# A gated Flamingo layer on one core: batch 0's first half in two quarters, with bonus sums by float32 matmuls

## What is computed

```python
def step(carry, kv_t):
    p, q, o = carry
    no = jnp.maximum(o, u + kt)
    A = jnp.exp(o - no); E = jnp.exp(u + kt - no)
    y = (A * p + E * vt) / (A * q + E)
    no2 = jnp.maximum(w + o, kt)
    A2 = jnp.exp(w + o - no2); E2 = jnp.exp(kt - no2)
    return ((A2 * p + E2 * vt, A2 * q + E2, no2), y)
...
x = x + tanh(g_xattn[0]) * wkv(4, 1024, 1024, w, u, layernorm(x), ctx_2048)
D = gelu(float16(layernorm(x)) @ W0.T + bias0).astype(float16)
x = x + tanh(g_ffn[0]) * (D @ W1.T + bias1).astype(float16)
```

## Time and profile before

| | us |
|---|---|
| median of three runs | 1918.29 (1917.05 to 1918.54) |
| the profiled execution, its own time | 1916.53 |
| its span, first to last instruction | 1914.7 |
| first group of half 0 starts | 112.13 |
| first group of half 1 starts | 240.16 |
| mean granted clock of TensorE | 0.998 |

### The profile page before, as it was taken

The page is one execution under the profiler, slowest core; times in us unless marked ns, Lnnn a source line. Parts: engine busy times, 40 slices in busy tenths (PEclk is TensorE's granted clock), DMA queues, the critical chain, the costliest instruction groups (busy, mean ns, idle before and its releaser), DMA issues.

```text
span 1914.7 us, 20205 instructions
## 1 busy us (share of the span) xinstructions
PE 1812.3 (95%) x8408; PEld 829.5 (43%) x8408; DVE 879.1 (46%) x997; ACT 555.7 (29%) x673; POOL 333.9 (17%) x325
## 2 busy tenths in 40 slices
PE   1189899999999999999999999999999999999999
PEld 0144444444444444444444444444444444444444
DVE  8968748898447857633215867742300000000000
ACT  5059534634424434311003434410101221100000
POOL 4336402565211211200001221200000000000000
PEclk9999999999999999999999999999999999999999
DMA  6639776767574443332452443233233212222330
GB/s 247 247 118 327 236 259 232 251 238 267 195 213 143 146 151 133 141 108 104 138 185 106 149 160 137 89 132 128 93 120 132 88 45 88 88 81 95 132 121 34
DMA packets 82953, 291.89 MB, mean 152 GB/s; under 512 B 12583, under 2 KB 12583, under 8 KB 75693
## 3 DMA queue, kind: packets, MB, share of 16 engines
q1 hardware_dynamic: 74940, 177.30, 27.3%
q10 hardware_dynamic: 7920, 113.30, 16.8%
HBM read 223.41 MB, written 67.16 MB: 152 GB/s over the span
## 4 chain that ended last, share of the span: by engine, by line
PE 90%; DVE 1%; ACT 1%; DMA 1%; POOL 1%; issue 1%; SPq 0%; ACTq 0%; DVEq 0%; POOLq 0%
PE accs L903 45%; PE accs L925 44%; POOL W L447 0%; DVE stats L626 0%; DMA var_dram<-tokens 0%; ACT W L555 0%; PE front L861 0%; PE back L870 0%; DMA total<-var_dram 0%; PE front L884 0%; DVE XT L757 0%; PE front L879 0%; DVE xh L673 0%; DMA var_dram<-total 0%; PE front L837 0%
## 5 line engine op out<-in xcount | busy, mean ns | idle before, releaser
L903 PE MATMUL accs<-XT,W 128*128 128x512 f16 x4096 | 888.9, 379 | 4.2 <-ACT XT L527 2.4
L925 PE MATMUL accs<-DT,W 128*128 128x512 f16 x4096 | 886.7, 379 | 0.0
L925 PEld LDWEIGHTS accs<-DT,W 128*128 128x128 f16 x4096 | 400.8, 98 | 487.3 <-issue 6.8
L903 PEld LDWEIGHTS accs<-XT,W 128*128 128x128 f16 x4096 | 400.8, 98 | 486.3 <-issue 5.1
L765 DVE SCALAR_TENSOR_TENSOR xo<-e,tg,xo 128x512 f32<-128x512 f16 x64 | 50.3, 787 | 633.0 <-ACT e L572 633.0
L564 ACT ACTIVATE DT<-accs,small 128x512 f16<-128x512 f32 x256 | 175.6, 686 | 516.0 <-PE accs L903 515.4
L572 ACT ACTIVATE e<-accs,small 128x512 f16<-128x512 f32 x64 | 43.9, 686 | 660.3 <-PE accs L925 660.3
L720 DVE RECIPROCAL S<-front 128x512 f32<-128x512 f32 x64 | 214.4, 3350 | 0.0
L425 POOL TENSOR_TENSOR X<-X,S 128x512 f32<-128x512 f32 x64 | 92.5, 1446 | 521.1 <-DVE S L723 521.1
L447 POOL TENSOR_TENSOR W<-stage,W 128x1024 f16<-128x1024 f32 x52 | 110.6, 2138 | 46.3 <-ACT stage L558 46.3
L706 DVE TENSOR_TENSOR front<-front,V 128x512 f32<-128x512 f32 x64 | 44.5, 696 | 137.6 <-ACT front L522 136.0
(11 more groups left out here) (69 smaller groups left out, 596.1 us busy)
## 6 DMA issues: line engine op xcount, KB each, us to landing
W<-parts_dram ACTq DMA_DIRECT2D x54, 2048.0 KB, 9.2
parts_dram<-W SPq DMA_DIRECT2D x64, 512.0 KB, 5.1
stage<-w_in SPq DMA_DIRECT2D x52, 512.0 KB, 5.7
xin<-x_in SPq DMA_DIRECT2D x32, 512.0 KB, 7.0
V<-vT_in SPq DMA_DIRECT2D x64, 256.0 KB, 5.5
X<-xT_in SPq DMA_DIRECT2D x64, 256.0 KB, 6.6
x_dram<-X SPq DMA_DIRECT2D x32, 512.0 KB, 4.5
xo<-x_dram SPq DMA_DIRECT2D x32, 512.0 KB, 4.3
```

The lines of the kernel that those rows point to most:

```text
L903: mm = nc.tensor.matmul(acc[m % BANKS], W[:, (nb // Q) % 2, part, nb % Q, P * c:P * (c + 1)], XT[:, c, HALF * half:HALF * (half + 1)], sta ...
L925: mm = nc.tensor.matmul(acc[m % BANKS], W[:, s % 2, part, q, P * c:P * (c + 1)], DT[:, nb, HALF * half:HALF * (half + 1)], start=(nb == 0 ...
```

## The change

The first half of batch 0 is worked as two quarters of 256 tokens (`QUARTER`). Units 0 to 7 are the first quarter, 8 to 15 the second, 16 to 23 the second half with 512 tokens.

- **First quarter.** The exp writes to SBUF (`EA`, in `total`), the product also (`EVA`). In place of DVE's two bonus sums TensorE forms them by four float32 matmuls of 256 columns: a diagonal matrix of the bonus (`diag`, made by ACT ahead of the first normalisation, 8 of 128x128) times E, plus the identity times the scan, and the same for the product (`terms`). DVE's order is scan, product, scan of unit n + 1 (`scans_first`), then reciprocal and quotient of unit n (`quotient_first`). 12 weight pieces are made ready beside it, 3 for each two units.
- **Matmul groups.** The first 64 groups (`EARLY`) have 256 columns: 25 of the first quarter, then, behind the second quarter's tiles (slot `SECOND` = 25), 12 of the second quarter, and then one of the first with two of the second in turn, to 64. The 32 groups of half 1 with 512 columns follow (slot `THIRD` = 64). `EXTRA` = 32 slots are added.
- **Tiles.** Their second normalisation stands between groups, not among them: tiles 0 and 1 ahead of slot 0, 2 and 3 at slot 25, 4 to 7 at slot 64. `xh` has two buffers.
- **Weight pieces.** More of them stay in the chip at first: in free parts of X2, XT, DT and W. Each is stored by two transfers, in an order of its own, with 8 semaphores.
- **Slots.** Units 8 to 15 in slots 1 to 13, units 16 to 23 in 31 to 61; POOL's residual has slots of its own (`ADD_SLOT`). Batch 1's units start three slots later in half 1 (43 in place of 40), the last is at the same place.

```diff
+QUARTER = HALF // 2
+LAG = 25
+EARLY = ([(0, nb) for nb in range(LAG)] + [(1, nb) for nb in range(12)] +
+         [x for j in range(NB - LAG) for x in ((0, LAG + j), (1, 12 + 2 * j), (1, 13 + 2 * j))] +
+         [(1, nb) for nb in range(12 + 2 * (NB - LAG), NB)])
+SECOND, THIRD = LAG, len(EARLY)
...
+WITH_UNIT = ((0, 1), (2,), (3, 4), (5,), (6, 7), (8,), (9, 10), (11,))
...
+            for c in range(CB):
+                nc.scalar.activation(diag[c], ident[:, :], ACT.Copy, scale=bonus[:, c:c + 1]).then_inc(diag_done, 1)
...
+            def scans_first(n):
+                j, w, c = n % 2, QUARTER, n
+                E, EV = EA[:, j, :], EVA[:, j, :]
+                S_p, S_q = S[:, j, 0, :], S[:, j, 1, :]
+                dve.wait_ge(seeded, n + 1)
+                dve.wait_ge(e_ready, n + 1)
+                nc.vector.tensor_tensor_scan(S_q[:, 1:w + 1], decay[:, c:c + 1].to_broadcast([P, w]), E,
+                                             S_q[:, 0:1], ALU.mult, ALU.add).then_inc(q_done, 1)
+                dve.wait_ge(v4_landed[n % 4], 16 * (n // 4 + 1))
+                if n >= 2:
+                    dve.wait_ge(nmm_done, n - 1)
+                nc.vector.tensor_tensor(EV, E, V4[:, n % 4, :], ALU.mult).then_inc(ev_done, 1)
+                dve.wait_ge(ev_done, n + 1)
+                nc.vector.tensor_tensor_scan(S_p[:, 1:w + 1], decay[:, c:c + 1].to_broadcast([P, w]), EV,
+                                             S_p[:, 0:1], ALU.mult, ALU.add).then_inc(p_done, 1)
+            def quotient_first(n):
+                dve.wait_ge(nmm_done, n + 1)
+                nc.vector.reciprocal(S_q, den).then_inc(rec_done, 1)
+                dve.wait_ge(rec_done, n + 1)
+                nc.vector.scalar_tensor_tensor(S_q, num, tg[:, 0:1], S_q, ALU.mult, ALU.mult).then_inc(y_done, 1)
...
+            def terms(n):
+                pe.wait_ge(diag_done, n + 1)
+                if n >= 2:
+                    pe.wait_ge(y_done, n - 1)
+                pe.wait_ge(e_ready, n + 1)
+                nc.tensor.matmul(den, diag[n], EA[:, j, :], start=True, stop=False)
+                pe.wait_ge(q_done, n + 1)
+                nc.tensor.matmul(den, ident[:, :], S[:, j, 1, 0:w], start=False, stop=True).then_inc(dmm_done, 1)
+                pe.wait_ge(ev_done, n + 1)
+                nc.tensor.matmul(num, diag[n], EVA[:, j, :], start=True, stop=False)
+                pe.wait_ge(p_done, n + 1)
+                nc.tensor.matmul(num, ident[:, :], S[:, j, 0, 0:w], start=False, stop=True).then_inc(nmm_done, 1)
...
             for n in range(CB):
-                unit(n)
+                if n + 1 < CB:
+                    scans_first(n + 1)
+                quotient_first(n)
...
+                    if K == SECOND:
+                        tokens_x2(2)
+                        tokens_x2(3)
+                        channels_x2(2)
+                        channels_x2(3)
+                    if K == THIRD:
+                        tokens_x2(4)
+                        for T in range(4, 8):
+                            if T < 7:
+                                tokens_x2(T + 1)
+                            channels_x2(T)
```

More of the change, by code:

```diff
@@ L153, in build @@
         xo = sb("xo", [P, 2, L])
+        lower, upper = e16[:, :, :].rearrange("p h t -> p (h t)").bitcast(F32), squares
+        diag = [(lower if c < 4 else upper)[:, P * (c % 4):P * (c % 4 + 1)] for c in range(CB)]
+        X2h = X2[:, :, :].bitcast(F16)
         ring = [stage[:, i, :] for i in range(RING2)] + [xo[:, i, :] for i in range(2)]
@@ L851, in tokens_x2 @@
[L851 to L859 removed]
+                ch, c = divmod(n, CB)
+                tiles = ((0, 1), (2, 3), range(HT, TILES))[ch]
+                if c == 0:
+                    pe.wait_ge(xn_ready, tiles[-1] + 1)
@@ new lines, in unit @@
+                if ch == 0:
+                    pe.wait_ge(e_ready, n - 1)
+                elif ch == 1 and c in (2, 3):
+                    pe.wait_ge(xh_ready, 2)
+                elif ch == 1 and c >= 4:
+                    pe.wait_ge(y_done, n - 3)
+                elif ch == 2 and c < 2:
+                    pe.wait_ge(xh_ready, 3 + c)
+                else:
+                    pe.wait_ge(y_done, n - 1)
+                for T in tiles:
+                    mm = transpose_piece(n, T)
+                mm.then_inc(kt_done, 1)
@@ L885, in variances, with group_early @@
                     .then_inc(var_done, 1)
+            def group_early(m):
+                quarter, nb = EARLY[m]
+                pe.wait_ge(lo_done, nb + 1)
+                if m >= BANKS:
+                    pe.wait_ge(acc_drained, m - BANKS + 1)
+                for c in range(CB):
+                    for part in range(2):
+                        mm = nc.tensor.matmul(acc[m % BANKS][:, 0:QUARTER], piece_block(nb, part, c),
+                                              XT[:, c, QUARTER * quarter:QUARTER * (quarter + 1)],
+                                              start=(c == 0 and part == 0), stop=(c == CB - 1 and part == 1))
+                mm.then_inc(mm_done, 1)
             def group1(b, k):
-                m = GROUPS * b + k
+                m = EXTRA + GROUPS * b + k
                 if b == 0:
                     half, nb = divmod(k, NB)
-                    if half == 0:
-                        pe.wait_ge(lo_done, nb + 1)
-                    elif nb % Q == 0:
+                    if nb % Q == 0:
                         pe.wait_ge(w_landed[(nb // Q) % 2], 16 * (nb // Q // 2 + 1))
```

601 lines of the change are left out of this document (377 added, 224 removed).

## The result

| | kernel before | changed kernel |
|---|---|---|
| median, us | 1918.2 (1917.05 to 1918.54) | 1951.58 (1950.43 to 1954.21) |
| profiled execution, its own time | 1916.53 | 1950.43 |
| span | 1914.7 | 1948.4 |
| first group of 256 or 512 columns starts | 112.13 | 89.36 |
| half 1 of batch 0 starts | 240.16 | 270.04 |

The account below looks back on a forecast made before the run. TensorE, 95% busy, bounds the kernel; half 1's start decides: 93.0 + 56.4 + 11.8 + 83.1 + 22.8 + 1.7 (clock) - 240.16 = +28.6 us on 1916.53, 1945.2, median about 1947. Range 1924 to 1955.

Parts of the forecast that it names:

- One number: The question reduced to when the matmuls of half 1 of batch 0 start (240.16 us before), and at which clock.
- A: Everything up to the first quarter's first matmul group, with scans and products taking turns with low parts: start at 93.0 us.
- Rival 1: In the first quarter only products take turns with low parts, scans do not: period 6.7, 1936.5 us; chance 0.15.
- rival 2: POOL and DVE don't meet at all: period 5.3, first group at 74.6, 1928.5 us; chance 0.13.
- The hand-off: First quarter: scans(n+2) wait for the seed POOL writes after quotient(n), a bare 1.1 us in each unit.
- TensorE's float32 work hidden: First quarter: the added float32 matmuls, 1.9 to 3.8 us a unit, are hidden in a period of 7.
- B: The first quarter's 25 matmul groups, until unit 15's residual is done: 56.4 us.
- C: The second quarter's tiles: statistics, normalisation, transposes and copy, all bare on TensorE, 11.8 us.
- E: Half 1's four tiles with no matmul group between them: 22.8 us.
- D: Half 1's units, DVE the slower side with 8 x 8.39 = 67.1 us, TensorE needing 59: 83.1 us in all.
- The later batches' numbers I price at nothing.: Moved stores, finer store waits and later batches cost nothing, since the matmuls behind 240 us hide them.
- rival 5: Worse: 2 us turns also catch x tiles' two-input steps, or batch 1's later units hold the means: 1955 and more; chance 0.06.

Follow-up runs that it names:

- a1_turns: The changed kernel with POOL's low parts of the first quarter held back until the next scans on DVE are done; 1941.8 us.
- a2_dvesums: The changed kernel with the first quarter's bonus sums back on DVE, exp and product in PSUM, no diagonal matrices, one unit after the other; 1927.25 us.
- a3_adds: The changed kernel with POOL's residuals of units 8 to 15 in earlier slots, residual 8 ahead of low part 16; 1952.93 us.
- a4_prep: The changed kernel with weight pieces 25 to 31 made ready in slots 33 to 45 in place of 34 to 52; 1948.82 us.
- a9_actfree: The changed kernel with ACT's work on weight pieces 13 and 14 moved ahead of its wait for tile 2's normalisation; 1951.96 us.
- a5: The changed kernel with batch 1's front earlier: first normalisation, most units and residuals 22 and 23 in earlier slots; 1951.56 us.
- the last kernel: The changed kernel with a2_dvesums, a3_adds, a4_prep, a5 and a9_actfree together, and other banks for half 1's four tiles; 1907.74 us, ratio 0.9939 to the kernel before.

## Why the prediction was right, and where it was off

The time was 1951.6 where 1947 was forecast, inside the range and for the reason given in the first quarter; in the sum for half 1's units a wait was missing. Point by point:

- **One number.** That all depends on half 1's start held for 29.9 of 33.7 us, and 1.8 more are the clock behind it (1.7 priced).
- **A, the turns.** Right in mechanism, and a1_turns shows it: scans and products are short once no low part lies beside them. Rival 1 (only products take turns) falls with the scans at 2129 ns, rival 2 with rows at 42.78 and 45.30. Off in size: 6.95 and 8.73 us for 7.35 and 9.5, since a scan that starts with a low part waits the rest of it, so that its 2.59 us hold only some 0.5 of its own 0.65. Three periods of each made 3.5 us of A's miss of 3.6. (The terms written for A add up to 82.35 + 10.15 = 92.5, not 93.0; by them the miss is 3.1.)
- **The hand-off.** 1.1 us expected, 1.00 and 1.09 in the rows. "I'm wrong if scans(n+2) start at once" didn't happen. What the prediction didn't do is to set its period against the 4.66 us of a unit whose sums stay on DVE, and its y(0) at 25.9 against one without matrices and without scans of unit 1 ahead: a2_dvesums shows the two at 4.64 and 20.0.
- **TensorE's float32 work hidden.** Yes, a pair of matmuls of 256 columns takes 0.7 us at the higher and 1.2 at the lower level of the clock, and TensorE waits for DVE between them.
- **B.** 56.5 against 56.4, but for part of the reason only. The seeds came late as worked out (unit 10: 3.75 us for 3.9; units 11 to 14: 4.8 for 5). The sentence "47 us if only TensorE counted" was wrong: with its waits for gelus it is 55.2. The seeds' waits come to 8.5 us in sum and are worth 1.3 (a3_adds).
- **C and E.** 12.0 for 11.8 and 22.4 for 22.8. TensorE stood 6.8 us ahead of E, not 9.
- **D.** The step that failed: "DVE is the slower side from here: 8 x 8.39". The first product was right to 0.2 us (172.69), but the sum took TensorE's 59 us as free of waits and never followed pieces 25 to 31, whose low parts are made three groups ahead of their use. 5.8 us, shown by a4_prep; the term came out 6.7 too small.
- **"The later batches' numbers I price at nothing."** Wrong by 2.0 us: rival 5's mechanism, that batch 1's units hold the means, is there in small. In the profiled executions of a3_adds and a9_actfree it took back what they gained.

The misses in A and in D were of opposite sign, and that is luck: the growth of the span was forecast at 28.6 us and measured at 33.7, 5.1 low, and without A's 3.6 it would have been nearly 9 low.

## What to carry to other kernels

Work moved to an idle engine brings its operands' place and its order with it. Here TensorE took 0.77 us a unit from VectorE, but wanted them in SBUF, where VectorE and GpSimd stand in each other's way, and put each seed's hand-off bare on the chain: price where operands lie and what now follows directly on what, before the work saved. And in a pipeline worked to within 1 or 2 us per stage, look for the second limit of each stage before crediting or dropping a repair: a3, a5 and a9 each removed or moved the wait they aimed at and gained nothing clear alone, and a2 to a5 gain 26 us one by one but 34.7 together. By the table most of that difference lies behind half 1's start, where a3 and a4 alone lost 6.8 and 2.1 us against the changed kernel.

Open is how much of the last kernel's 10 us the quarters earn: its banks and its slots were not tried on the kernel before.

## What the hardware showed

- A scan whose decay is one broadcast column and whose data lie in SBUF takes turns with a GpSimd subtraction from SBUF like an operation with two full SBUF inputs: 2.59 us where it takes 0.75 alone. With its data in PSUM it takes 0.74 beside the same low parts (a2_dvesums). The Trainium skill ("SBUF — State Buffer", Who interferes with whom) gives the rule for VectorE instructions with two SBUF inputs; the runs agree and show that it holds for such a scan.
- TensorE's granted clock behind a stage of short transposes comes up at different moments in different executions: in three kernels that are alike up to there it is 0.81, 0.81 and 0.50 at 160 to 163 us (changed kernel, a4_prep, a5_b1), and the first 64 matmuls take 8.74, 8.74 and 9.90 us.
- A wait of 3.55 us in a full stream brought the granted clock down to 0.50 and cost 2.0 us in the 96 matmuls behind it (a3_adds); one of 1.03 us left it at 1.00 (changed kernel).
